# The state-space block's output product from split halves of y and of its weights, with the low half of y made at the end of the slot

## The reference, cut to what matters

```python
zxbcdt = x @ W_in                                    # 256 -> 1160 columns
xBC = silu(causal_conv(xBC) + conv_b)                # 4 taps
ys = scan(step, s0, ...)                             # state 8 heads x 64 x 64
y = ys + D * x_ssm
y = y * silu(z)
y = y * rsqrt(mean(y * y, axis=-1) + EPS) * norm_weight   # 512 columns
return y @ W_out                                     # 512 -> 256
```

## Time and profile before

| what | us |
|---|---|
| median of 3 runs (lowest to highest) | 1296.35 (1295.36 to 1298.18) |
| the profiled execution | 1293.54 |
| its span, first to last instruction | 1291.8 |
| tile 0's mask, start of slot 0 | 453.6 |
| last router score copied, end of the middle block | 932.1 |

### The profile page before, as it was taken

The page is one execution under the profiler, slowest core; times in us unless marked ns, Lnnn a source line. Parts: engine busy times, 40 slices in busy tenths (PEclk is TensorE's granted clock), DMA queues, the critical chain, the costliest instruction groups (busy, mean ns, idle before and its releaser), DMA issues. The chain is left out here.

```text
span 1291.8 us, 21935 instructions
## 1 busy us (share of the span) xinstructions
PE 1031.2 (80%) x6500; PEld 859.2 (67%) x6532; DVE 751.1 (58%) x1619; ACT 605.3 (47%) x1558; POOL 608.5 (47%) x612
## 2 busy tenths in 40 slices
PE   3747999999934688888898899889548999999900
PEld 3746999999923556666666666666446999999900
DVE  6974444444427678787878777765283444444434
ACT  1324555555512355656456656555233555555500
POOL 6913555555421245454546454557305555555300
PEclk9998999999975699999999999999668999999955
DMA  6861222222232111111112100000152222222178
GB/s 227 277 276 50 77 77 78 76 77 78 63 115 74 37 29 41 42 42 41 42 41 62 42 25 18 17 25 25 40 242 70 75 78 79 75 78 78 53 249 282
DMA packets 73242, 112.20 MB, mean 87 GB/s; under 512 B 10664, under 2 KB 60336, under 8 KB 71856
## 3 DMA queue, kind: packets, MB, share of 16 engines
q1 hardware_dynamic: 47888, 58.77, 13.5%
q0 software_dynamic: 13824, 37.77, 9.1%
q10 hardware_dynamic: 11424, 14.30, 3.3%
HBM read 66.76 MB, written 44.04 MB: 86 GB/s over the span
## 5 line engine op out<-in xcount | busy, mean ns | idle before, releaser
L399 POOL DMA_INDIRECT ys_d<-xs,row_of x144 | 142.0, 986 | 193.9 <-DVE xs L779 188.1
L463 ACT ACTIVATE hs<-pH 128x512 f32<-128x512 f32 x144 | 86.1, 598 | 232.5 <-PE pH L581 232.5
L394 POOL DMA_INDIRECT xs<-xn_d,token_of x144 | 139.8, 971 | 115.0 <-DVE token_of L753 71.8
L768 DVE TENSOR_TENSOR xl<-pT,xh 128x256 fp32r<-128x256 f32 x144 | 61.2, 425 | 224.1 <-ACT xh L476 224.1
L773 DVE TENSOR_TENSOR h2l<-hs,h2h 128x512 fp32r<-128x512 f32 x144 | 99.8, 693 | 76.3 <-ACT h2h L471 76.0
L1557 DVE SCALAR_TENSOR_TENSOR acc<-bank,cwh,acc 128x511 f32<-128x511 f32 (+2 forms) x120 | 89.7, 747 | 43.4 <-ACT acc L1157 40.5
L601 PE MATMUL pY<-w2h,h2h 128*128 x576 | 103.0, 301 | 0.5 <-DVE h2l L773 0.3
L1057 POOL TENSOR_TENSOR yv<-yv,sz 128x512 f32<-128x512 f32 x32 | 40.7, 1273 | 117.2 <-DVE yv L1596 114.0
L581 PE MATMUL pH<-w1h,xh 128*128 x288 | 92.4, 403 | 1.8 <-DVE xl L768 1.1
L581 PE MATMUL pH<-w1l,xh 128*128 x288 | 92.3, 402 | 0.0
L601 PE MATMUL pY<-w2h,h2l 128*128 x576 | 92.2, 282 | 0.0
(11 more groups left out here) (248 smaller groups left out, 2562.2 us busy)
## 6 DMA issues: line engine op xcount, KB each, us to landing
m_yg<-ys_d SPq DMA_DIRECT2D x64, 128.0 KB, 2.2
xs<-ys_d SPq DMA_DIRECT2D x16, 512.0 KB, 5.8
wst<-in_L_ffn_w_dram ACTq DMA_DIRECT2D x8, 512.0 KB, 4.7
xs<-in_L_attn_x_dram SPq DMA_DIRECT2D x8, 512.0 KB, 6.3
hs<-in_L_ffn_w_dram ACTq DMA_DIRECT2D x8, 512.0 KB, 4.7
xn_d<-xs SPq DMA_DIRECT2D x8, 512.0 KB, 3.3
lo_d<-w1l SPq DMA_DIRECT2D x1, 4096.0 KB, 11.8
lo_d<-w2l SPq DMA_DIRECT2D x1, 4096.0 KB, 21.3
```

What stands on the lines that cost most here:

```text
L394: pool.indirect_dma_start(out=xg[:, t % NX, :], out_offset=None, in_=xn_d, in_offset=bass.IndirectOffsetOnAxis(ap=token_of[:, t:t + 1], ax ...
L399: pool.indirect_dma_start(out=ys_d, out_offset=bass.IndirectOffsetOnAxis(ap=row_of[:, t:t + 1], axis=0), in_=y[:, t % NX, :], in_offset=No ...
L463: act.activation(r[:, u, :], pH[u][:, :], ACT.Relu).then_inc(relu_done.sem, 1)
```

## The change

The output product is made from split operands. wo, scaled by the norm weights, is split once into woh and wol: ScalarE makes woh ahead of the slots (four instructions, in place of VectorE's four multiplications), VectorE makes wol at the end of prepare (four instructions). In each slot ScalarE's copy of y now writes the high half yTh (a copy to fp32r of the same size as before), and VectorE makes the low half yTl from the same bank, at the end of its slot, ahead of silu. out_product is twelve products of 256 columns (yTh x woh, yTh x wol, yTl x woh), and waits for yTl. turn_xc and turn_x2, which overwrite the bank, wait for VectorE's reading of it instead of ScalarE's.

```diff
-        yT = sb("yT", [P, KI, P])
+        yTh, yTl = sb("yTh", [P, KI, P], F32R), sb("yTl", [P, KI, P], F32R)
@@ scalar, weight preparation
+            for n in range(KI):
+                act.activation(woh[:, n, :], wo[:, n, :], ACT.Copy, scale=nw[:, n:n + 1]).then_inc(wo_hi, 1)
@@ scalar, copy_yT
-                act.activation(yT[:, :, :], by_head(pT[:, :], KI), ACT.Copy).then_inc(yT_copied.sem, 1)
+                act.activation(yTh[:, :, :], by_head(pT[:, :], KI), ACT.Copy).then_inc(yT_hi.sem, 1)
@@ tensor, out_product
-                pe.wait_ge(yT_copied.sem, yT_copied.done(i))
+                if i == 0:
+                    pe.wait_ge(wo_split, KI)
+                pe.wait_ge(yT_lo.sem, yT_lo.done(i))
-                product(pO[:, 0:D], [(yT[:, n, :], wo[:, n, :]) for n in range(KI)]).then_inc(o_ready.sem, 1)
+                product(pO[:, 0:D], [(a[:, n, :], w[:, n, :]) for a, w in ((yTh, woh), (yTh, wol), (yTl, woh)) for n in range(KI)]).then_inc(o_ready.sem, 1)
@@ tensor, turn_xc
-                pe.wait_ge(yT_copied.sem, yT_copied.done(i - 2))
+                pe.wait_ge(yT_lo.sem, yT_lo.done(i - 2))
@@ tensor, turn_x2
-                pe.wait_ge(yT_copied.sem, yT_copied.done(min(s, T - 1)))
+                pe.wait_ge(yT_lo.sem, yT_lo.done(min(s, T - 1)))
@@ vector, split_weights
-                for n in range(KI):
-                    link(dve.tensor_scalar(wo[:, n, :], wo[:, n, :], nw[:, n:n + 1], None, ALU.mult))
@@ vector, prepare
+                for n in range(KI):
+                    dve.wait_ge(wo_hi, n + 1)
+                    dve.scalar_tensor_tensor(wol[:, n, :], wo[:, n, :], nw[:, n:n + 1], woh[:, n, :].bitcast(F32), ALU.mult, ALU.subtract).then_inc(wo_split, 1)
@@ vector
+            def split_y(i):
+                dve.wait_ge(yT_hi.sem, yT_hi.done(i))
+                dve.wait_ge(o_ready.sem, o_ready.done(i - 1))
+                dve.tensor_tensor(yTl[:, :, :], by_head(pT[:, :], KI), yTh[:, :, :].bitcast(F32), ALU.subtract).then_inc(yT_lo.sem, 1)
@@ vector, the slot's end
                 if live(s + 9):
                     split_x(s + 9)
+                if live(s):
+                    split_y(s)
                 for B in blocks(s, TAPPED):
                     silu(*B)
```

More of the change, by code:

```diff
@@ L862, in mamba_block @@
         wih, wil = sb("wih", [P, KD, NIN], F32R), sb("wil", [P, KD, NIN], F32R)
-        wo = sb("wo", [P, KI, D])
+        wo, woh, wol = sb("wo", [P, KI, D]), sb("woh", [P, KI, D], F32R), sb("wol", [P, KI, D], F32R)
         cw, cb, nw = sb("cw", [P, NB, CONV]), sb("cb", [P, NB]), sb("nw", [P, KI])
@@ L923, in mamba_block @@
             step(n) for n in ("i", "y", "s", "s1", "S", "t1", "td", "t2", "yv", "sq"))
-        yT_ready, yT_copied, o_ready, xo_done = (step(n) for n in ("yT", "yT_copied", "o", "xo"))
+        yT_ready, yT_hi, yT_lo, o_ready, xo_done = (step(n) for n in ("yT", "yT_hi", "yT_lo", "o", "xo"))
+        wo_hi, wo_split = sem("m_wo_hi"), sem("m_wo_split")
         def row(G, n, k=0, chunks=GC):
@@ L1101, in _ @@
             for s in (al_done, norm_done, norm2_done, x2T_copied, logit_copied, xT_hi, tz_done, exp_u, exps, dec_out, h_saved, tap0, tb_done,
-                      xt_done, bt_done, ex0_done, ex_done, sq_done, yT_copied):
+                      xt_done, bt_done, ex0_done, ex_done, sq_done, yT_hi):
                 s.open(act)
@@ L1421, in _ @@
             for s in (add1, add2, stats, aggr, stats2, aggr2, var_done, nmr_done, xT_lo, sz_done, dt_added, soft, a_done, rest_done, cum_copied, decdt, dec_in,
-                      taps, xc_done, M_done, S_done, t1_done, t2_done, xo_done):
+                      taps, xc_done, M_done, S_done, t1_done, t2_done, xo_done, yT_lo):
                 s.open(dve)
```

## The result

The changed kernel takes 1334.96 us (median of 4 runs, 1333.61 to 1336.55), the kernel before 1297.26 us beside it (4 runs, 1295.36 to 1299.0). The ratio is 1.0268, with an interval from 1.0225 to 1.0311: slower, as forecast, but by 2.7% and not by 0.7%, and outside the range of 1299 to 1312. The profiled spans are 1333.3 us and 1291.8 us; the mean granted clock falls from 0.923 to 0.885.

A forecast was written before the change was run, and what follows sets the result against it. It took a path passing between TensorE and VectorE, set by who is late at each slot boundary, as the bound. 7.1 + 0.7 + 1.4 - 1.3 + 0.8 = +8.7 us on 1296.35 gave 1305.1 us, range 1299 to 1312.

The forecast's parts named there:

- The late slots: Slots 27 on: nothing hides turn_x2's wait, +0.73 less 0.32 for the shorter product; +0.41 each for three slots.
- phase 2 to 3: Boundary where turn_x2 is 1.09 us late, but add_second's and silu's stalls cover it: cost 0, except +0.7 for slot 15.
- The sum: All forecast terms added, at +8.7 us on the kernel before.
- the preparation: Before the slots: wil begins 0.8 us earlier, wol's four subtractions add 1.6 us; +0.8 us in all.
- Phase 3 to 0: Boundary where turn_x2 waits for the subtraction, delaying the cumulative sums: five times 1.25 us and once 0.91, +7.1 us.
- Rival 4: More low clock from TensorE's added idle time: two to four more stretches on the sum, 1308.7 to 1312.3 us; chance 0.10.
- Rival 1: Hidden after all: a later stall takes up phase 3's lateness, 1298 us; chance 0.12.
- Rival 2: VectorE becomes the bound: its 0.60 us show at every boundary if the gate stops waiting, at most 1316 us; chance 0.10.
- Rival 3: Faster: turn_x2 has its bank in time and TensorE's shorter product decides, 1293 us, down to 1287; chance 0.06.
- B: Theory of the follow-up runs: the lighter product, twelve short instructions for eight long ones, brings the clock down by itself.

The follow-up runs named there:

- e4: Changed kernel plus eight 512-column products, results unread, ahead of turn_x2 in phase 3; 1314.75 us, ratio 1.0103.
- e2: Kernel before, with its four f32 products, plus the change's subtraction (result unused) and its waits; 1332.0 us, ratio 1.0254.
- e3: Changed kernel without the subtraction and its waits; still twelve products, the last four reusing the high half of y; 1298.47 us, ratio 0.9966.
- e10: Changed kernel with cumulative sums ahead of turn_x2, turn_x2 writing the output product's bank, five unused products ahead of the sums; 1293.52 us, ratio 0.9899.
- e1: Changed kernel, but in phase 3 VectorE makes the low half of y inside the softplus chain; 1323.61 us, ratio 1.0164.

## Why the prediction was wrong

**Right: the place and the size at the high clock.** turn_x2 waits for VectorE's new line at five of six boundaries of phase 3, at three of seven of phase 2 (slots 6, 14 and 22) and from slot 27 on. A slot of phase 0 at the full clock takes 17.5 us (16.5 before) and a group of four, in e4, 63.1 us against 61.9: +1.2, forecast 1.25. The late slots take 11.3 us instead of 10.9, forecast +0.41. Timeline of after, slot 27's end:

```profile
913.15 0.62 ACT L1197 ACTIVATE yTh<-bank 128x512 fp32r<-128x512 f32 x1
...
913.80 0.69 DVE L1514 TENSOR_TENSOR yTl<-bank,yTh 128x512 fp32r<-128x512 f32 x1
...
914.59 0.41 PE L1376 MATMUL bank<-ident,m_xn 128*128 128x128 f32 x2 [0.80 <-issue]
...
916.90 0.72 PE L1258 MATMUL bank<-woh,yTh 128*128 128x256 f32 x4
...
918.38 0.89 PE L1282 MATMUL bank<-xdt,ex 128*128 128x64 f32 x7
```

turn_x2 stands 1.44 us after the start of ScalarE's copy, 0.72 before: forecast +0.73. The product, 916.90 to 918.38, takes 1.48 us, forecast 1.49. So the twelve loads cost nothing beyond the pace of the expert block's row, and the bound that the prediction drew from the rule on the fast load of weights (Trainium skill, "TensorE: Matmul & The Clock Gate", section "Weight-path perf modes — Fast Weight Load (FWL) and DoubleRow"), no gain, was not met: the product gained 0.33 us.

**Right in its cover, wrong in its cost: phase 2 to 3.** Timeline of after, slot 6 into 7:

```profile
569.54 0.68 DVE L1580 SCALAR_TENSOR_TENSOR acc<-tb,acc 128x512 f32<-128x512 f32 x1
569.72 0.41 PE L1376 MATMUL bank<-ident,m_xn 128*128 128x128 f32 x2 [0.95 <-issue]
...
576.27 0.48 DVE L1602 SCALAR_TENSOR_TENSOR xo<-bank,m_rstd,xr 128x256 f32<-128x256 f32 x1 [3.32 <-PE bank L1258]
576.67 0.47 DVE L1465 SCALAR_TENSOR_TENSOR xr<-m_yg,gates,xr 128x256 f32<-128x256 f32 x1
```

silu takes 0.68 us instead of 1.27: the subtraction went into its stall, as forecast. add_second takes 0.47 and not the 0.8 that I said would show, since this slot is at the low clock and its product, 3.32 us waited for, comes after GpSimd's instruction. In slot 19 of e4, at the full clock, it takes 0.74 us. The same windows view of after, for that low clock:

```profile
572.00:585.70 13.70, 13.70 (x58) 11.38 (x58) 7.75 (x25) 4.87 (x16) 5.90 (x9) 0.50 0.16 50
```

It begins 2.3 us behind turn_x2's gap of 0.95 us, and slot 7 takes 18.2 us instead of 14.4. The sum had 0 for it. In slots 15 and 23, both at the full clock, VectorE waits 1.44 and 1.83 us for the product, where it waited 0.61 and 1.00 before, and the slots take 1.4 and 1.2 us more; the sum had 0.7 for slot 15 and nothing for slot 23, which has no add_second there to cover it. With slot 3 (2.1 us more, with 2.5 us of low clock) these are most of phase 3's 9.3 us. Phase 2 gave back 1.6 us over its slots and phase 1 took 1.4.

**Right in its parts, not in its sum: the preparation.** Its two rows:

```profile
386.35 2.77 DVE L1441 TENSOR_TENSOR wil<-acc,wih 128x1160 fp32r<-128x1160 f32 x2 [1.29 <-ACT wih L1109]
...
397.92 1.67 DVE L1454 SCALAR_TENSOR_TENSOR wol<-wo,nw,woh 128x256 fp32r<-128x256 f32 x4
```

wil starts 1.30 us earlier than before (forecast 0.8), wol takes 1.67 (forecast 1.6), and tile 0's mask starts 0.1 us earlier, not 0.8 later. So the 0.8 us show nowhere in the time at which tile 0 starts.

**The step that failed: "Phase 3 to 0", and with it "Phase 2 to 3".** The first priced the lateness as a shift of 1.25 us, 7.1 in all, at an unchanged clock. The sum moved idle time onto TensorE and did not ask what TensorE does after it. Measured, phase 0 took 31.7 us more. About 6 of these are the shift, five times 1.2; the rest is low clock. A slot of phase 0 with 14 us of it takes 22.8 instead of 17.5 us, 5.3 more, or 0.38 us for each us at 1.2 GHz. After has 95.5 us more of low clock in its slots than before, an estimate of 36 us. The shifts at the full clock are some 8 us (the 6, 2.6 in slots 15 and 23, 1.2 in the late slots, less phase 2's 1.6). That makes 44 against 41.5 measured, so by this estimate the clock is more than four fifths of the loss. "Phase 2 to 3" was put at 0 for the same reason: its cover holds at an unchanged clock, and slot 7 lost 3.8 us to the low clock behind it.

**Rival 4 named the mechanism and missed its price twice.** I gave it 0.10 and two to four stretches at 1.79 us each, the product's own loss in slot 31. There were six stretches of 10 to 17 us, and each slows all that TensorE does in the slot, its projections and the sums of the state too, so it costs 5.3 us. The row that I took was one instruction where the stretch was the unit. With the five stretches of phase 0 at 5.3 us on top of the sum, known only afterwards, the forecast would have been 1331.6 us.

**The other rivals.** Rival 1: phase 3's lateness was not hidden (1.2 of 1.25 us show in e4's group). Rival 2: the gate did not stop waiting. The waits view of after, 473 to 990 us:

```profile
DVE xo L1602 <- PE bank L1258: 23.4, 15, 5.1
DVE sz L1504 <- ACT tz L1143: 23.3, 22, 2.3
```

The gate waits 23.3 us in all for tanh of z, 25.7 before. The 16.5 us for the product there end at 925 us and leave out the last tile's wait, 6.36 us at 926.2; over the whole block it was 22.8 us before and is 23.4 now. Rival 3: turn_x2 had its bank late at five of six boundaries of phase 3, by far more than 0.32 us.

**What stays open.** e2 shows that the subtraction and its waits suffice, and e4 that TensorE's idle time is the way by which most of it acts. In the table 23 of the 39 boundaries with over 1 us of idle time have low clock, and none of the 33 without it. B is not settled: e3 has the gap of before and more low clock than its profile, but e3's time is the same and the kernel before itself ran from 1293 to 1312 us over the series, and no run varied the product's length at a fixed gap often enough to tell. Nor do these profiles say which idle time brings the clock down. It fell at 4 of 13 boundaries with 1.1 to 1.3 us, at 6 of 11 with 1.3 to 1.5, at 5 of 5 with 1.6 to 1.7 and at 8 of 10 with 2.0 to 2.6. There is one profile of each version, while the runs of one version differ by up to 1.4%. And the kernel before's own profile was one of its faster executions (span 1291.8 us; e10's is 1293.3 us), so e10's 1.0% over many runs may be mostly a gain in steadiness.

## What to carry to other kernels

When a change makes TensorE wait a microsecond longer, price the microsecond and then what the clock may do behind it: add the new wait to the idle time that already stands there, look for a row of the same kernel with a whole stage at the low clock, and take the difference of stages, not of instructions. If work can't be moved into the gap, a few products that nothing reads are worth trying (20 us here for eight of them per group); they helped only at the place where they stood, so look at every gap that the change makes longer. And where a second reader of a PSUM bank makes the next writer late, move the writer to another bank before moving the reader.

## What the runs showed of the hardware

- A stretch of 6.8 us in which TensorE was busy 4.33 us, with a single gap of 2.47 us, stood before 13.7 us at 1.2 GHz. The granted clock stayed at 0.5 although TensorE was then busy without a break. The Trainium skill has such short idle times between groups of products as a cause of a clock that goes to and fro ("TensorE: Matmul & The Clock Gate", section "A second HAM failure mode: psum-queue depth-cycling"); the traces agree in this, with 112.6 us of low clock in the slots after the change.
- In one profile (e2), gaps of 2.59 and 2.58 us had 10 us of low clock behind them and another of 2.58 us had none, so the length of one gap alone does not decide it. Gaps of 0.38 to 0.49 and 1.22 us close together (e1) went with low clock at five of five boundaries, a single one of 1.19 to 1.31 us (before and e3) at four of twelve.
- Twelve fp32r products of 256 columns in 1.48 us from start to the next start: 0.123 us each, loads included. Four f32 products of the same size took 1.81 us.
